# Graph network: the score operand turned as f32 and split out of PSUM, and the opening re-ordered

## What is computed

```python
h = jnp.maximum(_layernorm(x, axis=-1), 0.0)
# layer 0
norms = jnp.maximum(jnp.linalg.norm(x, axis=-1), COS_EPS)        # x is h here
sim = x @ x.T / (norms[:, None] * norms[None, :])
attn = jax.nn.softmax(beta * sim * adj, axis=1)
return diffusion + jax.nn.sigmoid(alpha) * (attn @ x - x)        # diffusion: dis * adj * dis @ x - x
```

## Time and profile before

| | us |
|---|---|
| median of 3 runs | 914.65 (913.48 to 915.18) |
| the profiled execution, its own time | 914.35 |
| its span in the profile | 912.6 |
| TensorE busy in the span | 851.5 (93%) |
| VectorE busy | 617.4 (68%) |
| ScalarE busy | 490.7 (54%) |
| GpSimd busy | 276.2 (30%) |

### The profile page before, as it was taken

One profiled execution on the slowest core, in us unless ns is written; L12 is line 12 of the kernel. 1 busy time (PEld: TensorE's weight loads), 2 busy tenths in 40 slices (PEclk: granted clock), 3 DMA queues, 4 the chain that ended last, 5 costly groups with the idle time before them and its releaser, 6 DMA issues.

```text
span 912.6 us, 18173 instructions
## 1 busy us (share of the span) xinstructions
PE 851.5 (93%) x6496; PEld 510.1 (56%) x6496; DVE 617.4 (68%) x1655; ACT 490.7 (54%) x1027; POOL 276.2 (30%) x253
## 2 busy tenths in 40 slices
PE   0489999999999999999999999999999999999992
PEld 0256777777777777654444455555455555555451
DVE  6999989898999999962445413323046676637776
ACT  3869888888988887641222211111055556434543
POOL 4585434343444354422212100000022231213221
PEclk9999999999999999999999999999999999999997
DMA  8899999999999996000000000000000000000000
GB/s 263 208 202 223 240 259 234 289 231 262 254 262 258 237 257 141 2 1 1 1 1 1 0 1 1 1 1 1 1 1 1 1 1 1 1 1 24 24 24 24
DMA packets 96079, 89.77 MB, mean 98 GB/s; under 512 B 74369, under 2 KB 79617, under 8 KB 96001
## 3 DMA queue, kind: packets, MB, share of 16 engines
q1 hardware_dynamic: 92352, 88.11, 41.3%
q10 hardware_dynamic: 3648, 0.61, 0.4%
HBM read 69.81 MB, written 2.10 MB: 79 GB/s over the span
## 4 chain that ended last, share of the span: by engine, by line
PE 73%; DVE 11%; issue 6%; ACT 4%; POOL 2%; DVEq 2%; DMA 1%; ACTq 1%; POOLq 0%
PE ps_acc L1358 29%; PE ps_acc L1269 16%; PE ps_s L1251 11%; PE ps_t L1358 7%; PE ps_t L1251 5%; DVE e_parts L814 2%; POOL att_sb L397 2%; PE ps_s L1420 2%; DVE ps_s L807 1%; DMA cols<-in_L_gnn_beta 1%; PE ps_s L1388 1%; ACT e_parts L625 1%; ACT adj_t L479 1%; ACTq L461 1%; DVE ez L1124 1%
## 5 line engine op out<-in xcount | busy, mean ns | idle before, releaser
L1269 PEld LDWEIGHTS ps_acc<-h_a,e_parts 128*128 128x128 f16 x3072 | 185.7, 97 | 37.7 <-DVE e_parts L814 7.7
L1269 PE MATMUL ps_acc<-h_a,e_parts 128*128 128x129 f16 x3072 | 197.4, 219 | 5.3 <-DVE e_parts L814 5.1
L1358 PE MATMUL ps_acc<-adj_t,stage 128*128 128x512 fp8e4 x896 | 198.9, 379 | 0.0
L340 POOL CAST e_parts<-ez 128x1024 f16<-128x1024 f32 x128 | 139.1, 1086 | 189.9 <-PE ps_acc L1269 96.5
L1358 PE MATMUL ps_acc<-adj_t,h_a 128*128 128x512 fp8e4 x768 | 170.3, 379 | 0.0
L814 DVE TENSOR_TENSOR e_parts<-ez,e_parts 128x1024 f16<-128x1024 f32 x128 | 157.8, 1234 | 17.8 <-POOL e_parts L340 15.9
L1358 PEld LDWEIGHTS ps_acc<-adj_t,stage 128*128 128x128 f16 x896 | 87.1, 98 | 98.9
L1251 PE MATMUL ps_s<-u_t 128*128 128x512 f16 x534 | 133.3, 388 | 7.5 <-ACT u_t L485 5.0
L470 ACT ACTIVATE bytes<-stage 128x1024 uint8<-128x1024 f32 x128 | 133.9, 1046 | 0.9 <-DVE x L775 0.6
L496 ACT ACTIVATE ez<-ps_s,scal 128x1024 f32<-128x1024 f32 x89 | 107.1, 1204 | 45.8 <-DVE ps_s L807 44.4
L584 ACT ACTIVATE ez<-x,small 128x128 f32 (+1 forms) x96 | 39.6, 482 | 159.7 <-DVE small L982 159.7
(11 more groups left out here) (158 smaller groups left out, 829.8 us busy)
## 6 DMA issues: line engine op xcount, KB each, us to landing
stage<-in_adj SPq DMA_DIRECT2D x128, 512.0 KB, 5.0
x<-in_x SPq DMA_DIRECT2D x4, 512.0 KB, 8.2
adj_t<-bytes SPq DMA_TRANSPOSE x128, 5.1
out<-x SPq DMA_DIRECT2D x8, 256.0 KB, 2.2
kernel_sb<-in_L_gnn_kernel ACTq DMA_DIRECT2D x1, 64.0 KB, 7.0
w_sb<-in_L_gnn_W ACTq DMA_DIRECT2D x1, 64.0 KB, 8.2
embed_top<-in_L_gnn_embed ACTq DMA_DIRECT2D x1, 64.0 KB, 8.3
embed_top<-in_L_gnn_layer ACTq DMA_DIRECT2D x1, 64.0 KB, 7.5
```

What stands on the lines that cost most here:

```text
L340: g.tensor_copy(e_parts[:, HI, at:at + 2, :], ez[:, at:at + 2, :]).then_inc(ehi_done, 1)
L1269: last = t.matmul(att_acc[:, b, 0:D + 1], e_parts[:, re, g_s % RING, P * b:P * (b + 1)], h_a[:, s, rh, 0:D + 1], start=(s == 0 and n == 0 ...
L1358: last = t.matmul(acc, h[:, k, r, :], adj_f8[:, k // 2, CW * c:CW * (c + 1), k % 2], start=(k == 0 and r == LO), stop=(k == NB - 1 and r = ...
```

## The change

The u halves are made on the other side of the transpose. VectorE only scales u in f32 (`scale_u`), TensorE transposes the f32 blocks (4 transposes for a quarter in place of 8), ScalarE writes the f16 high half (512 columns), and VectorE makes the low half out of PSUM (`low_ut`). GpSimd no longer makes a low half of u; it now casts h to its high half (`high_h`), which VectorE did. The lists of all four engines are re-ordered, ScalarE's wait for the last parameter transfer comes later, and four entries of the small-step tables grow by one.

```diff
-W_AFTER = (W_0, W_1, [15, 20, 29, 35, 46, 51, 61, 67], [24, 26, 33, 35, 41, 49, 57, 64])
-T_AFTER = ((), (), [20, 25, 36, 41, 52, 57, 68, 73], ())
+W_AFTER = (W_0, W_1, [15, 20, 29, 35, 46, 51, 61, 67], [24, 26, 33, 35, 42, 49, 57, 64])
+T_AFTER = ((), (), [20, 25, 37, 41, 53, 57, 69, 73], ())
...
-            def low_u(q):
-                pool.wait_ge(u_hi_ok, q + 1)
-                g.tensor_tensor(quarter(u0p, q)[:, :, :, LO, :], quarter(u0f, q),
-                                quarter(u0p, q)[:, :, :, HI, :], ALU.subtract).then_inc(u_ok, 1)
+            def high_h(q):
+                pool.wait_ge(relu_ok, q + 1)
...
+                g.tensor_copy(dst[:, :, :, HI, :], h0f[:, 2 * q:2 * q + 2]).then_inc(hi_ok, 1)
...
-                a.activation(u_t[:, :, CW * q:CW * (q + 1)],
-                             ps_t16[:, q % 2, :].rearrange("p (r i) -> p r i", r=2), ACT.Copy
-                             ).then_inc(ut_ok, 1)
+                a.activation(u_t[:, HI, CW * q:CW * (q + 1)], ps_t[:, q % 2, :], ACT.Copy
+                             ).then_inc(ut_hi_ok, 1)
...
-            def high_u(q):
+            def scale_u(q):
...
-                                .broadcast_to([P, 2, 2, D]), ALU.mult)
-                dve.drain()
-                v.tensor_copy(u0p[:, cs, :, HI, :], u0f[:, cs]).then_inc(u_hi_ok, 1)
+                                .broadcast_to([P, 2, 2, D]), ALU.mult).then_inc(u_ok, 1)
+
+            def low_ut(q):
+
+                dve.wait_ge(ut_hi_ok, q + 1)
+                cols_q = slice(CW * q, CW * (q + 1))
+                v.tensor_tensor(u_t[:, LO, cols_q], ps_t[:, q % 2, :], u_t[:, HI, cols_q],
+                                ALU.subtract).then_inc(ut_ok, 1)
...
-                for k in range(BC * q, BC * (q + 1)):
-                    for r in (LO, HI):
-                        last = t.transpose(dst[:, r, P * (k % BC):P * (k % BC + 1)],
-                                           u0p[:, k // 2, k % 2, r, :], ident16[:, :])
+                for k in range(BC * q, BC * (q + 1)):
+                    last = t.transpose(ps_t[:, q % 2, P * (k % BC):P * (k % BC + 1)],
+                                       u0f[:, k // 2, k % 2, :], ident32)
```

More of the change, by code:

```diff
@@ L349, in _ @@
             rstd0(1)
+            high_h(0)
+            low_h(0)
+            high_h(1)
             rstd0(2)
-            low_h(0)
+            norm_u(0)
             low_h(1)
-            norm_u(0)
+            high_h(2)
             rstd0(3)
-            low_u(0)
+            high_h(3)
+            low_h(2)
             norm_u(1)
-            low_u(1)
-            low_u(2)
-            low_u(3)
+            low_h(3)
+            high_h(4)
+            low_h(4)
+            high_h(5)
+            low_h(5)
             norm_u(2)
+            high_h(6)
+            low_h(6)
             high_pair(0)
-            low_u(4)
+            high_h(7)
+            low_h(7)
             high_pair(1)
             norm_u(3)
[L365 to L380, removed]
+            for p in range(2, 9):
+                high_pair(p)
             for c in range(NCH):
@@ L867, in _ @@
             stats0(2)
-            high_h(0)
-            high_h(1)
+            scale0(1)
+            square_h(0)
+            square_h(1)
             norm0_in(0)
-            scale0(1)
-            beta_columns()
             scale0(2)
             stats0(3)
-            high_h(2)
-            high_u(0)
-            high_h(3)
-            high_u(1)
+            square_h(2)
+            scale_u(0)
+            scale_u(1)
+            square_h(3)
             norm0_in(1)
             scale0(3)
-            high_h(4)
-            high_h(5)
-            high_u(2)
-            high_u(3)
+            low_ut(0)
+            beta_columns()
+            square_h(4)
+            low_ut(1)
+            scale_u(2)
+            scale_u(3)
+            square_h(5)
             norm0_in(2)
+            low_ut(2)
+            square_h(6)
             z_pair(0)
+            low_ut(3)
             z_pair(1)
-            high_h(6)
-            high_h(7)
-            high_u(4)
+            scale_u(4)
+            low_pair(0)
+            z_pair(2)
+            square_h(7)
             norm0_in(3)
-            z_pair(2)
-            low_pair(0)
+            scale_u(5)
             low_pair(1)
             z_pair(3)
-            high_u(5)
+            low_ut(4)
             low_pair(2)
             z_pair(4)
-            high_u(6)
+            low_ut(5)
             low_pair(3)
             z_pair(5)
+            scale_u(6)
+            low_pair(4)
             z_pair(6)
-            low_pair(4)
-            high_u(7)
+            scale_u(7)
             low_pair(5)
             z_pair(7)
+            low_ut(6)
             low_pair(6)
@@ L909, in _ @@
             low_pair(7)
+            low_ut(7)
             gate_columns()
@@ L1288, in _ @@
             scores(2)
+            turn_u(4)
             scores(3)
-            turn_u(4)
             att_pair(0)
+            turn_u(5)
+            att_pair(1)
             scores(4)
-            att_pair(1)
+            att_pair(2)
             scores(5)
-            att_pair(2)
-            turn_u(5)
-            scores(6)
             att_pair(3)
             turn_u(6)
+            scores(6)
+            att_pair(4)
             scores(7)
-            att_pair(4)
+            att_pair(5)
+            turn_u(7)
             scores(8)
-            att_pair(5)
             att_pair(6)
-            turn_u(7)
             scores(9)
```

75 lines of the change are left out of this document (34 added, 41 removed).

## The result

| | us |
|---|---|
| changed kernel, median of 4 runs | 906.68 (906.31 to 907.55) |
| kernel before, 4 runs beside it | 914.15 (913.48 to 915.18) |
| ratio | 0.9912, 95% interval 0.9892 to 0.9931 |
| profiled execution, time and span | 906.31 and 904.5 (before 914.35 and 912.6) |

The forecast was 907.4. The profiled execution is 8.0 us shorter than the one before, its span 8.1.

What follows compares the result with a forecast made beforehand. VectorE and the engines in front of it bound the first 75 us, TensorE the rest; 914.35 - 6.8 (opening) - 0.2 (small steps) = 907.35, forecast 907.4 us, 8-in-10 range 904.9 to 911.3.

Steps and rivals of the forecast that it cites:

- What bounds the opening: First 75 us: VectorE and the engines in front of it bound the kernel; the gain is TensorE idle time removed.
- The terms: Per-operation costs: low half 0.60 us, GpSimd cast of h 0.55, ScalarE copy pitch 0.50, four f32 transposes 1.2 early, 0.60 later.
- The rule weighed: VectorE instructions with at most one SBUF input, outside two-port modes, don't contend with GpSimd, freeing the new low half.
- the other case: The low half out of PSUM collides with GpSimd as well: walk gains 0.8 us less, sum 908.2.
- Steps 1 to 3 of the walk: Opening: first scores 7.1 us earlier (26.3), first attention product 4.4 earlier (43.6), pair 8 at 71.3; 6.8 us taken.
- the walk: Opening: the four engines' lists stepped through in order, each instruction starting after its engine, releaser and any collision.
- most of the 7 us is lost again: Opening: first adj product starts at about 36.2 us for 37.05, losing most of the first scores' 7.1 us gain.
- The pairs: Pairs 0 to 8: 27.7 us from 43.6 to 71.3, where the walk of the old lists took 29.0.
- the tables: Layers 2 and 3, small steps one quarter later: most removed waits come back; 0.2 us gained for both.
- The dear cast: Rival, opening: GpSimd's cast of h costs 1.1 us, not 0.55; walk loses 3.4 us, 910.8; chance 0.17.
- The tables in full: Rival, layers 2 and 3: chains move with TensorE, 2.5 us gained in place of 0.2, 905.1; chance 0.09.
- Slower, the low half at 1.2 us: Rival, opening: each low half costs 1.2 us and collides with GpSimd's casts; 1.3 us later, 915.7; chance 0.06.

Runs made afterwards that it cites:

- experiment 9: Changed kernel with each low half out of PSUM done twice, the extra one into an unused place: 910.41 us.
- experiment 10: Changed kernel with GpSimd's cast of h done twice, the first overwritten: 909.68 us.
- experiment 2: Changed kernel with the four small-step table entries put back to their old values: 907.42 us.
- experiment 4: Kernel before with only ScalarE's wait for the last parameter moved behind relu of quarter 5: 914.19 us beside 913.89.
- experiment 1: Kernel before with only the four table entries of the change: 914.42 us beside 913.89, ratio 1.0005.
- experiment 12: Changed kernel with another order of the opening on all four engines and step 5 of layer 3 one quarter later: 897.9 us, ratio to before 0.9818.
- experiments 7: Kernel before with only the new u path (f32 turn, split out of PSUM), old order and old cast of h: 918.12 us beside 917.25.
- 8: Changed kernel's order, cast of h on GpSimd and tables, with the old u path put back: 923.66 us beside 914.05.
- the third order: Changed kernel with the same operations in another order of the opening on all four engines: 899.35 us, ratio to before 0.9803.
- experiments 5: Changed kernel with the cast of h back on VectorE, ahead of the sums of squares: 909.17 us.
- 3: Changed kernel with ScalarE's wait for the last parameter put back ahead of relu of quarter 2: 909.7 us.
- 6: Kernel before with only the cast of h moved to GpSimd, ahead of each low half of h: 918.62 us beside 917.25.

## Why the prediction was right, and where not

**What bounds the opening: right in the main.** VectorE and what stands ahead of it: experiments 9 and 10 show both VectorE and GpSimd on the path. In experiment 2's execution the path also went through TensorE, whose third turn stands behind the slow first scores. Of the delays that were no work, the prediction named ScalarE's 3.11 us and left out VectorE's 1.78 us for the same transfer (experiment 4).

**The terms.** The low half's pitch is 0.59 (25.27 to 25.86) for 0.60; two copies out of PSUM take 1.05 us together for 2 x 0.50; eight f32 transposes after idleness 1.94 for 2.4, four later ones 0.66. The cast of h has a pitch of 0.68 (13.39 to 14.07) for 0.55, so about 1 us more of GpSimd over the eight; experiment 10 shows that this direction costs.

**The rule weighed: the trace agrees.** The low half out of PSUM keeps its 0.68 to 0.69 us beside a busy GpSimd while the squares stretch to 1.17. The Trainium skill (SBUF — State Buffer, Who interferes with whom) says that only VectorE instructions that need the shared ports contend; the eight low halves agree with it, so the other case, priced at 0.8 us, did not arise.

**Steps 1 to 3 of the walk.** First scores right. The first adj product came 1.9 us earlier than walked and everything up to the first attention product with it (1.7 us): "most of the 7 us is lost again" was too gloomy, 2.8 us of it got through. The pairs gave 0.7 us of that back (28.4 us for 27.7). The size of the sum, 6.8 as the middle between 5.8 and 7.6 (which is 6.7), hit 6.73 in the profiled execution. Experiment 2 with the same opening gives 5.83, and the pieces erred by 1.7 us one way and 0.7 the other, so that precision was luck.

**The step that was mis-sized: the tables.** The prediction took 0.2 us for both layers. The layers' late part gained 1.42 us. Two things were wrong. First, in layer 2 I read the room before `prepare` at one chunk (719.57 to 719.73) and used it for three. In the third chunk before the change, the copy ended at 788.58 and `prepare` began at 789.51, 0.9 us of room, and the wait went there in full; in the second it went too. That is 0.72 for 0.15. Second, I held VectorE's chain to be fixed apart from TensorE. It moved with the opening's change: by 0.4 us in experiment 2, and in layer 3 the wait before step 5 is 0.90 with the new opening where it is 1.42 with the old (experiment 1). For layer 3's own table entry the reasoning was right: alone it gains nothing.

**The rivals.** The dear cast was priced right (3.4 for a measured 3.0). The tables in full did not come; with another order and one more entry (experiment 12) none of the four waits is left. "Slower, the low half at 1.2 us": at twice its length (experiment 9) the kernel is still 3.6 us faster than before, so the length alone would not have made it slower. A low half that also collides was not run. The walk is too dear on the old list (by 1.8 us) and in experiment 9 (7.7 for 3.7), and too cheap in experiments 7 and 8.

## What to carry over

In a start-up phase written as in-order lists, look for what stands ahead of the first consumer on the engine that all later work waits for: the third order, in which the first adj product stands four steps earlier, was worth nearly as much again as the whole change. (All four lists moved there, and no run moves these four steps alone.) A wait for a transfer belongs behind all work that does not need it, on every engine that waits: moving ScalarE's alone gained nothing while VectorE still waited for the same landing, and putting it back in the new order cost 3.0 us. And price a moved small step at every place where it occurs, since the room behind it differs from place to place.

## What was not expected of the hardware

**A stall of VectorE that goes with the instruction count.** In layer 3 VectorE has idle stretches of about 0.4 us that no releaser ends: one in the changed kernel, two in experiment 1 (the other at 879.99), three in experiment 9. The first of each, in the timeline of VectorE, experiment 1 (old lists), changed kernel, experiment 9:

```profile
862.28 0.16 DVE L1177 TENSOR_TENSOR att_sb<-att_sb 128x4 f32<-128x4 f32 x1 [0.44 <-issue]
```

```profile
854.61 0.17 DVE L1026 TENSOR_SCALAR att_sb<-att_sb 128x4 f32<-128x4 f32 x1 [0.39 <-issue]
```

```profile
856.61 0.16 DVE L1188 TENSOR_TENSOR att_sb<-att_sb,cols 128x4 f32<-128x4 f32 x1 [0.45 <-issue]
```

In the changed kernel it falls behind the product (L1190 there) that ScalarE waits for, and step 5 of layer 3 waits 0.90 us. With eight instructions more on VectorE in the opening (experiments 5 and 9) it falls ahead of that product, and step 5 waits 1.2 us. Experiments 2, 3 and 10 to 12, with as many VectorE instructions as the changed kernel, have it at the same instruction as that one. Experiments 5 to 9, each with eight more (drains counted), all have it at one other instruction, two ahead of the product, and the old lists, with sixteen more, at a third, further ahead. What the stall is the traces don't say; that its place moves with the number of instructions ahead of it on its engine, they show. So an edit in the opening can cost or gain 0.2 to 0.5 us at a wait far behind it.

**The first scores at two speeds.** The same 12 matmuls took from 3.88 to 5.30 us in different executions, among them 4.61, 4.77 and 5.03: 0.44 us each where all twelve ran at half of TensorE's speed (5.30), 0.23 at full (2.76 for twelve), and times in between where the change-over fell inside them. TensorE had been idle for 22 us and more before its first transposes. The clock column does not show it in so short a stretch (1.00 over 25.84 to 31.10 of experiment 2), the lengths do. The same lists reached pair 8 up to 0.9 us apart, so single openings cannot be compared to better than that.
